# Global attention's two products in halves of f16, odd heads' probabilities scaled on ScalarE, and a new table of begin times

## What is computed

```python
# global part, per example
q, k = rope(x@w_q), rope(x@w_k)
scores = einsum('bqd,bkd->bqk', q, k) / sqrt(256)      # causal
y = einsum('bqt,btd->bqd', softmax(scores), v)
# local part, two layers: each row of a 128-row window looks at its own and the previous window
sim = einsum('bhwid,bhwjd->bhwij', 8*q, k)              # masked, 8 heads
o = einsum('bhwij,bhwjd->bhwid', softmax(sim), v)
x = x + o @ wo
x = x + (a * gelu(g)) @ w2 + b2                         # [a, g] = layernorm(shift(x)) @ w1 + b1
```

## Time and profile before

| what | value |
|---|---|
| median of 3 runs | 2738.49 us (2735.34 to 2739.82) |
| the profiled execution's own time | 2740.08 us |
| its span, first to last instruction | 2738.3 us |
| busy share: PE, DVE, ACT, POOL | 95%, 86%, 63%, 48% |
| mean granted TensorE clock | 0.987 |

### The profile page before, as it was taken

How to read it: one execution, slowest core, us unless ns; L and a number is a source line. 1 busy time by engine, 2 the same in 40 slices (tenths; PEclk the granted TensorE clock), 3 DMA queues, 4 the chain that set the end, 5 groups by cost and what they waited for, 6 DMA issues and landing times.

```text
span 2738.3 us, 70254 instructions
## 1 busy us (share of the span) xinstructions
PE 2598.4 (95%) x25086; PEld 1758.4 (64%) x25086; DVE 2357.1 (86%) x7207; ACT 1730.4 (63%) x4172; POOL 1309.5 (48%) x953
## 2 busy tenths in 40 slices
PE   6999989999899998999999998999999999999997
PEld 4666656666566665666656665666656666666665
DVE  7988978989899887988879888898878989889895
ACT  3477744777457764667646685467763777537774
POOL 2465534555345543555335553355544555335552
PEclk8999999999999999999999999999999999999999
DMA  6000010000100000000000000000000000000000
GB/s 204 1 9 6 6 41 2 7 7 10 36 3 6 8 18 27 4 10 4 20 24 5 9 6 23 20 6 8 6 22 20 6 8 6 23 20 6 7 6 21
DMA packets 51016, 46.37 MB, mean 17 GB/s; under 512 B 11530, under 2 KB 47980, under 8 KB 50548
## 3 DMA queue, kind: packets, MB, share of 16 engines
q1 hardware_dynamic: 50004, 40.78, 4.9%
q10 hardware_dynamic: 672, 1.10, 0.1%
HBM read 25.06 MB, written 8.42 MB: 12 GB/s over the span
## 4 chain that ended last, share of the span: by engine, by line
PE 63%; DVE 15%; issue 5%; ACT 4%; POOL 4%; DMA 2%; DVEq 0%; POOLq 0%; ACTq 0%
PE ps L158 13%; PE ps L159 12%; PE ps L160 12%; PE ps L559 6%; PE ps L526 4%; PE ps L543 4%; PE ps L449 4%; PE ps L503 3%; DMA rows<-xu 2%; PE ps L404 2%; DVE ar_b L1039 2%; DVE ar_b L1055 1%; DVE small L992 1%; PE ps L468 1%; POOL small L1304 1%
## 5 line engine op out<-in xcount | busy, mean ns | idle before, releaser
L765 ACT ACTIVATE ar_b<-ar_b,small 128x192 f32<-128x192 f32 (+1 forms) x1024 | 446.3, 438 | 104.4 <-DVE small L1039 101.9
L1304 POOL TENSOR_TENSOR small<-small,neg_half 128x16 f32<-128x16 f32 x128 | 386.0, 3016 | 181.8 <-DVE small L997 177.7
L1308 POOL TENSOR_TENSOR ar_c<-ar_c 128x1024 f32<-128x1024 f32 x128 | 309.4, 2417 | 227.4 <-DVE ar_c L1025 225.4
L1039 DVE CUSTOM_DVE_ANT_0 ar_b<-ps,mask_t,small 128x192 f32<-128x192 f32 x896 | 321.1, 411 | 13.1 <-PE ps L526 11.1
L158 PE MATMUL ps<-wqkv_hi,ht_hi 128*128 128x512 f16 x768 | 293.1, 382 | 2.5 <-DVE ht_lo L987 2.4
L291 POOL TENSOR_SCALAR stats<-stats 128x2 f32<-128x2 f32 x128 | 34.9, 273 | 542.4 <-DVE stats L1087 263.1
L159 PE MATMUL ps<-wqkv_lo,ht_hi 128*128 128x512 f16 x768 | 291.8, 380 | 0.0
L160 PE MATMUL ps<-wqkv_hi,ht_lo 128*128 128x512 f16 x768 | 291.6, 380 | 0.0
L158 PE MATMUL ps<-ht_hi,w_hi 128*128 128x512 f16 (+1 forms) x704 | 273.3, 388 | 11.7 <-DVE ht_lo L987 11.7
L1055 DVE TENSOR_SCALAR ar_b<-ar_b,rsw 128x192 f32<-128x192 f32 (+1 forms) x1024 | 274.4, 331 | 9.5 <-DVE rsw L1048 0.4
L159 PE MATMUL ps<-ht_lo,w_hi 128*128 128x512 f16 (+1 forms) x704 | 272.1, 387 | 0.0
(11 more groups left out here) (185 smaller groups left out, 6596.7 us busy)
## 6 DMA issues: line engine op xcount, KB each, us to landing
xu<-in_L_attn_x_dram SPq DMA_DIRECT2D x32, 256.0 KB, 2.9
out_dram<-xu SPq DMA_DIRECT2D x64, 128.0 KB, 2.7
rows<-xu SPq DMA_DIRECT2D x128, 63.5 KB
mlp<-in_L_ffn_wqkv_dram SPq DMA_DIRECT2D x2, 1536.0 KB, 14.8
modb<-mod_rows SPq DMA_DIRECT2D x8, 384.0 KB, 5.8
rows<-in_L_ffn_w_dram SPq DMA_DIRECT2D x2, 1364.0 KB, 10.9
rows<-xu SPq DMA_DIRECT2D x112, 0.5 KB
ar_b<-in_L_wmod_dram SPq DMA_DIRECT2D x2, 768.0 KB, 7.5
```

The costliest lines, as they stand in the source:

```text
L765: last = act.activation(pw, pw, ACT.Exp, bias=mnw[:, n % 2, h:h + 1], scale=-1.0, accum_out=smw[:, n % 2, h:h + 1])
L1039: last = dve.tensor_tensor_reduce(out=PW[:, pw_at(f, q, i) + c:pw_at(f, q, i) + KW], in0=ps[:, bk, i * KW + c:(i + 1) * KW], in1=mask, sca ...
L1304: pool.tensor_tensor(rinv[:, n % 4, :], ssm[:, n % 2, :], neg_half[:, 0:16], ALU.pow).then_inc(s_rinv, 1)
L1308: pool.tensor_tensor(M1[:, n % 2, :], M1[:, n % 2, :], M2, ALU.add).then_inc(s_add, 1)
```

## The change

**1. Global products.** `QK1`, `V1` and `PT1` become pairs of f16 arrays in the same bytes. The copies `qc` and `vc` now write the high half on ACT, and new pieces `ql` and `vl` on DVE subtract it from the PSUM bank to give the low half. For the probabilities the new piece `ph` on ACT writes the high half and `pc` on DVE becomes the subtraction. `sc` and `av` use `mm3`. The banks are free only after `ql`, `vl` and `pc`.

**2. Odd heads.** `nm` on DVE forms the reciprocal of the four sums and scales two heads, the even ones. The new piece `na` on ACT scales the two odd ones. `H` waits for both.

**3. Begin times.** All tables are new; `PERIOD` goes from 323.83 to 316.98.

```diff
-        QK1 = ar_a[:, 0:4096].rearrange("p (c s n) -> p c s n", c=NC, s=2)
+        QK1 = [ar_a[:, 2048 * i:2048 * i + 2048].bitcast(F16).rearrange("p (c s n) -> p c s n", c=NC, s=2)
+               for i in range(2)]
...
                     elif k == "sc":
                         b, i = ids
-                        pe.wait_ge(s_qk, at("qc", b, i))
+                        pe.wait_ge(s_ql, at("ql", b, i))
...
-                                pe.matmul(ps[:, bk + kb, 0:w], QK1[:, c, 0, i * P:(i + 1) * P],
-                                          QK1[:, c, 1, kb * 512:kb * 512 + w], start=(c == 0), stop=(c == 1))
+                                mm3(pe, ps[:, bk + kb, 0:w], [q[:, c, 0, i * P:(i + 1) * P] for q in QK1],
+                                    [q[:, c, 1, kb * 512:kb * 512 + w] for q in QK1], c == 0, c == 1)
...
                         for kb in range(i + 1):
-                            last = pe.matmul(ps[:, bk, 0:DIM], PT1[:, i % 2, kb, :], V1[:, kb, :],
-                                             start=(kb == 0), stop=(kb == i))
+                            last = mm3(pe, ps[:, bk, 0:DIM], [q[:, i % 2, kb, :] for q in PT1],
+                                       [q[:, kb, :] for q in V1], kb == 0, kb == i)
...
                     elif k == "H":
                         n, f = ids
                         pe.wait_ge(s_pn, at("nm", n, f))
+                        pe.wait_ge(s_pa, at("na", n, f))
...
+                    elif k == "ph":
+                        b, i, k4 = ids
+                        act.wait_ge(s_ptr, at("pt", b, i, k4))
...
+                        act.activation(PT1[0][:, i % 2, 4 * k4:4 * k4 + m, :],
+                                       ps[:, bank["pt", b, i, k4], 0:m * P].rearrange("p (k n) -> p k n", n=P),
+                                       ACT.Copy).then_inc(s_ph, 1)
...
+                    elif k == "na":
+                        n, f = ids
+                        act.wait_ge(s_rsw, at("nm", n, f))
+                        act.wait_ge(s_exp, at("ex", n, f, 1))
+                        c = 0 if n % NT else HQ
+                        for i in range(2):
+                            h = 4 * f + 1 + 2 * i
+                            pw = PW[:, pw_at(f, 1, i) + c:pw_at(f, 1, i) + KW]
+                            last = act.activation(pw, pw, ACT.Copy, scale=rsw[:, n % 2, h:h + 1])
+                        last.then_inc(s_pa, 1)
...
+                    elif k == "vl":
+                        b, t = ids
+                        dve.wait_ge(s_v1, at("vc", b, t))
...
+                        dve.tensor_tensor(lo, src, hi, ALU.subtract).then_inc(s_vl, 1)
+                    elif k == "ql":
+                        b, t = ids
+                        dve.wait_ge(s_qk, at("qc", b, t))
+                        hi, lo = (q[:, :, :, t * P:(t + 1) * P] for q in QK1)
+                        dve.tensor_tensor(lo, ps[:, bank["qt", b, t], :].rearrange("p (c s n) -> p c s n", c=NC, s=2), hi,
+                                          ALU.subtract).then_inc(s_ql, 1)
...
                         for q in range(2):
                             dve.wait_ge(s_exp, at("ex", n, f, q))
+                        if n >= 2:
+                            dve.wait_ge(s_pa, at("na", n - 2, f))
                         dve.reciprocal(rsw[:, n % 2, 4 * f:4 * f + 4], smw[:, n % 2, 4 * f:4 * f + 4]).then_inc(s_rsw, 1)
...
-                        for q in range(2):
-                            for i in range(2):
-                                h = 4 * f + q + 2 * i
-                                pw = PW[:, pw_at(f, q, i) + c:pw_at(f, q, i) + KW]
-                                last = dve.tensor_scalar(pw, pw, rsw[:, n % 2, h:h + 1], None, ALU.mult)
+                        for i in range(2):
+                            h = 4 * f + 2 * i
+                            pw = PW[:, pw_at(f, 0, i) + c:pw_at(f, 0, i) + KW]
+                            last = dve.tensor_scalar(pw, pw, rsw[:, n % 2, h:h + 1], None, ALU.mult)
...
-PERIOD = 323.83
+PERIOD = 316.98
```

More of the change, by code:

```diff
@@ L93, in adaln_kernel @@
         ar_a = sb("ar_a", [P, 24 * 256])
-        QK1 = ar_a[:, 0:4096].rearrange("p (c s n) -> p c s n", c=NC, s=2)
-        V1 = ar_a[:, 4096:6144].rearrange("p (t n) -> p t n", t=NT)
+        QK1 = [ar_a[:, 2048 * i:2048 * i + 2048].bitcast(F16).rearrange("p (c s n) -> p c s n", c=NC, s=2)
+               for i in range(2)]
+        V1 = [ar_a[:, 4096 + 1024 * i:5120 + 1024 * i].bitcast(F16).rearrange("p (t n) -> p t n", t=NT) for i in range(2)]
         V = ar_a[:, 0:2048].rearrange("p (r n) -> p r n", r=4)
@@ L101, in adaln_kernel @@
         P1 = ar_b[:, 0:2048].rearrange("p (r n) -> p r n", r=2)
-        PT1 = ar_b[:, 2112:4160].rearrange("p (r k n) -> p r k n", r=2, k=NT)
+        PT1 = [ar_b[:, 2112 + 1024 * i:3136 + 1024 * i].bitcast(F16).rearrange("p (r k n) -> p r k n", r=2, k=NT)
+               for i in range(2)]
         PW = ar_b[:, 0:2112]
@@ L170, in adaln_kernel @@
                                          sem("h_lo_ready"))
+        s_ql, s_vl, s_ph = sem("qk_lo_ready"), sem("v_lo_ready"), sem("probsT_hi_ready")
         s_proj, s_m1a, s_v1, s_rot = sem("proj_done"), sem("rope_products"), sem("v_copied"), sem("rope_done")
@@ L238, in empty @@
             if k == "pj":
-                return s_v1, at("vc", *ids)
+                return s_vl, at("vl", *ids)
             if k == "qt":
-                return s_qk, at("qc", *ids)
+                return s_ql, at("ql", *ids)
             if k == "sc":
@@ L930, in _ @@
                         dve.tensor_scalar(nm1[:, i:i + 1], mx1[:, i:i + 1], -GAMMA, None, ALU.mult).then_inc(s_nm, 1)
+                    elif k == "vl":
+                        b, t = ids
+                        dve.wait_ge(s_v1, at("vc", b, t))
+                        bk = bank["pj", b, t]
+                        src = ps[:, bk:bk + 2, 2 * P:3 * P].rearrange("p c (d h) -> p d c h", h=HPC)
+                        hi, lo = (q[:, t, :].rearrange("p (d c h) -> p d c h", c=NC, h=HPC) for q in V1)
+                        dve.tensor_tensor(lo, src, hi, ALU.subtract).then_inc(s_vl, 1)
[5 more added lines that the diff above has]
+                                          ALU.subtract).then_inc(s_ql, 1)
                     elif k == "pc":
                         b, i, k4 = ids
-                        dve.wait_ge(s_ptr, at("pt", b, i, k4))
-                        if i >= 2:
-                            dve.wait_ge(s_y, at("av", b, i - 2))
-                        elif b:
-                            dve.wait_ge(s_pv, at("I", last_n(b), 1))
+                        dve.wait_ge(s_ph, at("ph", b, i, k4))
                         m = min(4, i + 1 - 4 * k4)
-                        dve.tensor_copy(PT1[:, i % 2, 4 * k4:4 * k4 + m, :],
-                                        ps[:, bank["pt", b, i, k4], 0:m * P].rearrange("p (k n) -> p k n", n=P)
-                                        ).then_inc(s_pte, 1)
+                        hi, lo = (q[:, i % 2, 4 * k4:4 * k4 + m, :] for q in PT1)
+                        dve.tensor_tensor(lo, ps[:, bank["pt", b, i, k4], 0:m * P].rearrange("p (k n) -> p k n", n=P), hi,
+                                          ALU.subtract).then_inc(s_pte, 1)
                     elif k == "ys":
@@ new lines @@
+    ("bw", "pe"): {(0, 0): -7.46, (0, 1): 2.64, (0, 2): 8.25, (0, 3): 12.59, (1, 0): 40.81, (1, 1): 45.54,
+        (1, 2): 47.41, (1, 3): 48.84},
+    ("co", "act"): {(0,): -15.41, (1,): 27.89},
+    ("cq", "act"): {(0, 0): 2.68, (0, 1): 6.61, (1, 0): 45.3, (1, 1): 70.45},
+    ("cv", "act"): {(0,): -0.64, (1,): 46.67},
+    ("cw", "act"): {(0, 0): -6.21, (0, 1): 0.82, (1, 0): 31.73, (1, 1): 51.89},
+    ("do", "dve"): {(0,): -13.19, (1,): 29.82},
+    ("dq", "dve"): {(0, 0): 6.25, (0, 1): 8.34, (1, 0): 50.99, (1, 1): 103.49},
@@ new lines @@
+    ("dv", "dve"): {(0,): 1.11, (1,): 85.3},
+    ("dw", "dve"): {(0, 0): 10.54, (0, 1): 21.57, (1, 0): 36, (1, 1): 60.87},
+    ("z0", "dve"): {(): -30.17},
+    ("zM", "pe"): {(): -21.4},
+    ("zR", "pe"): {(): -23.65},
+    ("zT", "pe"): {(): -27.43},
+    ("zW", "pe"): {(): -18.05},
+    ("za", "act"): {(): -30.17},
+    ("zb", "sp"): {(): -5.02},
+    ("zc", "sp"): {(): -29.7},
+    ("zd", "act"): {(): -22.56},
+    ("ze", "act"): {(): -26.54},
+    ("zf", "dve"): {(0,): 19.32, (1,): 53.25},
@@ new lines @@
+    ("zg", "sp"): {(): -21.69},
+    ("zh", "act"): {(): -18.51},
+    ("zi", "dve"): {(): -26.32},
+    ("zk", "dve"): {(): -19.57},
+    ("zl", "dve"): {(): -17.64},
+    ("zm", "sp"): {(): -7.6},
+    ("zn", "dve"): {(): -17.81},
+    ("zo", "sp"): {(0,): -26.98, (1,): -26.5},
+    ("zp", "dve"): {(): -22.56},
+    ("zq", "sp"): {(0,): -7.3, (1,): 10.18},
+    ("zr", "act"): {(): -11.57},
+    ("zs", "sp"): {(): 10.7},
+    ("zt", "dve"): {(): -10.36},
+    ("zu", "dve"): {(): -20.44},
+    ("zv", "sp"): {(0,): -25.48, (1,): 16.46},
@@ L1573 @@
+    ("zw", "sp"): {(0,): -26.02, (1,): 23.63},
```

(3 more changed lines are left out.)

57 lines of the change are left out of this document (11 added, 46 removed), and 691 rows, old and new, of tables (BEGIN, EDGE).

## The result

The changed kernel takes **2666.91 us** (median of 4 runs, 2665.09 to 2670.74) where the kernel before took 2738.06 beside it: a ratio of 0.9743, 95% interval 0.9726 to 0.976, so 71 us less. The forecast was 2686.5, range 2668 to 2708. The sign is right; the time lies 1 us under the range, in rival (b). The profiled execution took 2665.09 us.

What follows compares the result with a forecast made beforehand. The prediction took TensorE's matmul stream as the bound, except where chains through other engines hold it up. Its terms, -60 + 11 + 0 - 4 + 1 = -52 us, against 2738.5 gave 2686.5 us, range 2668 to 2708.

Steps and rivals of the forecast that it cites:

- rival (b): Freed VectorE gives more than forecast: Term 4 at its lower end, 2655 to 2668 us; chance 6%.
- What bounds the kernel: Whole kernel: TensorE's matmul stream, busy 95% of the span, is the bound, except where a chain through other engines holds it up.
- Term 1: Score and output products as f16 passes stream faster than f32: -60 us, between -55 and -64, with 2 us allowed for narrow passes.
- Term 2: Hand-offs: global products also wait for VectorE's subtractions after ScalarE's copies: +11 us, from -10 to +35.
- Term 3: Odd heads' scaling moved from VectorE to ScalarE; neither becomes the bound: 0 us, between -7 and +20.
- Rival (c): `na` waits for VectorE's reciprocal and blocks ScalarE's queue: 0.3 us for each of 256 pieces, +77 us, 2763 us; chance 5%.
- Term 4: New order: +1 us an example in the global part, -1.5 outside as VectorE is freed: -4 us, between -32 and +24.
- terms 3 and 5: The odd heads' move to ScalarE, 0 us, and two more table loads on ScalarE, +1 us.
- Signs: What would show the forecast right: period, global part and rest, engine busy times, multiplications, and low-half waits near 20 us.
- Table loads: Two more table loads of 1.28 us on ScalarE: +1 us, 0 to 2.6.

Runs made afterwards that it cites:

- relief_old: The kernel before with the odd heads left unscaled, in the old order, so VectorE is freed of 512 multiplications and ScalarE gets nothing: 2725.07 us (ratio 0.9949).
- new_without_halves: The changed kernel with the f32 products of before taken back, without low halves, in the new order: 2716.5 us (ratio 0.9919).
- new_no_chain: The changed kernel with high halves multiplied three times, TensorE waiting only for ScalarE's copies except at an example's last tile; subtractions still done: 2669.14 us (ratio 0.9744).
- n_work: The kernel before, odd heads unscaled, old order, with two scratch copies on ScalarE, awaited by nobody, just behind each `nm` of an odd head: 2820.4 us (ratio 1.0317).
- n_wait: The kernel before, odd heads unscaled, old order, with ScalarE only waiting for VectorE's reciprocal at those 256 places, doing no work: 2727.7 us (ratio 0.9956).

## Why the prediction was wrong by a little, point by point

- **What bounds the kernel.** TensorE's stream, except where a chain through other engines holds it up: this held, but the exception was priced too low. 14 us came from relief of VectorE with the same matmuls (`relief_old`), and 95 could be lost by 256 pieces of 0.69 us on ScalarE, whose share never passed 75%.
- **Term 1, -60.** Passes and distances came out as read (0.215 and 0.11 us), so by them the products are shorter by what was worked out, and 2 us more since the narrow passes weren't slowed. TensorE's busy time falls by 60 from `new_without_halves` (2593.2 us) to the changed kernel. What of this reaches the kernel's time can't be measured without the hand-offs.
- **Term 2, +11.** Waits at the low halves rose from 10 to 24 us, as forecast ("near 20"). But taking the waits away gains nothing (`new_no_chain`), so this mechanism was worth about 0 in the new order (with the clock, 9 at most) and 35 in the old. Terms 1 and 2 together: -49 forecast, -50 measured; since the mechanism of term 2 didn't cost its 11 us, the agreement of the sum is partly luck. What takes 10 of the 60 us instead isn't settled. An estimate from two rows of runs: 111 us less busy time on VectorE gave 14 us, and the subtractions add 69 us there, which by the same rate is 9; nothing was run that shows it.
- **Term 3, 0.** 1.5 us paid on ScalarE in the changed kernel: right. Rival (c) set 0.3 us a piece for a blocked ScalarE; in the old order a piece did cost 0.37 us. But the cause is ScalarE's work in its in-order list (`n_work`), where the rival had its wait for the reciprocal, which costs nothing (`n_wait`). The rule on multiplying on VectorE, not ScalarE (the Trainium skill, page "ScalarE: Activation LUTs", section "Rules for kernel authors") is right on the duration (440 ns against 250) and wrong on this kernel: undoing the move costs 85 us in the order that was made for it.
- **Term 4, -4: the step that failed.** It was the right mechanism with the wrong size: -22 measured (with terms 3 and 5, which are 1 or 2 us), -14 by VectorE's relief in the old order and -8 by the new order. I had set +1 us an example in the global part and -1.5 outside. Measured against the kernel before, the rest fell by 7 us an example (265 to 258), of which the products explain about one, and the global part by 4 where 1 to 4 were forecast. In the global part VectorE was expected at 66.5 us of work and was busy 62.7. The lower limit taken, half of TensorE's 8.6 us of idle in the rest, was read from *idle* time; of the 7 us only 1.8 came out of idle (8.6 to 6.9) and 5.2 out of time shown as busy (256.4 to 251.2). About one of these is the products; another 1.7 can be the granted clock: before, each of three such stretches has 3.4 us at the lower level, the like stretches now have none, though over the whole execution the clock didn't rise.
- **Signs.** Period 323 to 324 (327 forecast), global part 65 (65 to 68), rest 258 (259 to 262), VectorE 2274 (2295), ScalarE 1932 (2000), multiplications 512. Each is at the edge or beyond, on one side, though the rest stays 1 us above the bound set for rival (b): the lower end of term 4 was given 6%, and the row that spoke for it, 19.4 + 14.1 + 6.6 us of waits for VectorE, was weighed too lightly. They are 16.7, 11.3 and no row after.
- **Table loads, +1.** 112 of 1283 ns, as said; too small to be seen.

## What to carry to other kernels

When a kernel's order is fitted to its work, a change of the work and a change of the order can't be priced apart: each alone may lose what both together win, and a kernel with one part taken out tells about the order that it is left in as much as about the part. When work moves from the fuller to the emptier of two in-order engines, look for the gap in the receiving list at that very place (here 0.69 us of work against an estimated 0.8 or 1.5 us of room on average), not at its busy share. And read what relief of a second engine may bring from TensorE's time between starts, not from its idle time, which hides pauses shorter than the stretch by which a matmul's modelled end reaches past the next start. A row of waits is no price either: take the wait away and see what comes in its place, and compare the granted clocks before you name a cause.

## What the hardware showed that I had not expected

- 0.69 us of independent work on ScalarE, for which nobody waits, costs 0.37 us of the kernel's time each of 256 times with ScalarE 66% busy; 2.8 us later in the list it costs 0.10.
- A wait of ScalarE for VectorE's reciprocal at the same 256 places costs 0.01 us each, not to be told from nothing.
- f16 passes of 128 columns start 0.056 us apart though each loads its own weights for 0.10 us: the loads overlap each other. Timeline of TensorE's weight loads in the changed kernel, at the scores of tile 0:

```profile
1019.04 0.10 PEld L162 LDWEIGHTS ps<-ar_a 128*128 128x128 f16 x1
1019.09 0.10 PEld L160 LDWEIGHTS ps<-ar_a 128*128 128x128 f16 x1
1019.15 0.10 PEld L161 LDWEIGHTS ps<-ar_a 128*128 128x128 f16 x1
```
